# The preparation of a linear layer's weights in three float32r passes instead of one f32 pass, with GpSimd and VectorE splitting the operands

## The reference, cut to what matters

```python
x = x + L0(x)   # one expert per batch row (argmax of cond_8): silu(x wu + bu) * (x wg + bg), then wd, bd
x = x + L1(x)   # x W_base^T + b_base + 2 * sum_e cond[b,e] * (x As[e]^T) Bs[e]^T
x = x + L2(x)   # below
x = x + L3(x)   # two experts per batch row, weighted, gelu(x g) * (x u) then d; and a shared expert

def _L2_cond_ref(x, y, weight, mask, bias):
    masked_w = weight * mask[None, :, :]
    w_bot = jnp.einsum('bg,got->bot', y, masked_w)
    return jnp.einsum('bnt,bot->bno', x, w_bot) + bias
```

## Time and profile before

| | |
|---|---|
| median of 3 runs | 153.5 us (153.43 to 153.65) |
| the profiled execution | 153.69 us, of which 151.7 us are the span of its instructions |
| TensorE (PE) busy | 147.4 us, 97% of the span |
| VectorE (DVE) busy | 109.8 us, 72% |
| ScalarE (ACT) busy | 72.0 us, 47% |
| GpSimd (POOL) busy | 91.4 us, 60% |

### The profile page before, as it was taken

The page is one execution under the profiler, slowest core; times in us unless marked ns, Lnnn a source line. Parts: engine busy times, 40 slices in busy tenths (PEclk is TensorE's granted clock), DMA queues, the critical chain, the costliest instruction groups (busy, mean ns, idle before and its releaser), DMA issues.

```text
span 151.7 us, 3108 instructions
## 1 busy us (share of the span) xinstructions
PE 147.4 (97%) x1075; PEld 135.1 (89%) x1075; DVE 109.8 (72%) x229; ACT 72.0 (47%) x138; POOL 91.4 (60%) x93
## 2 busy tenths in 40 slices
PE   7999999999999999999999999999999999999992
PEld 2479999999978999999989999999999999999881
DVE  3985666667996586867775967876587895968772
ACT  2875444461375554454444354545425434345640
POOL 1003999999700007849994939995876999880000
PEclk9999999999999999999999999999999999999999
DMA  2999999974354676393397386095447047000052
GB/s 62 414 401 403 411 405 394 420 298 144 154 190 138 175 160 225 78 302 109 78 309 252 130 269 215 0 300 206 190 134 280 4 139 274 4 4 0 0 209 72
DMA packets 13912, 30.15 MB, mean 199 GB/s; under 512 B 1337, under 2 KB 8009, under 8 KB 13769
## 3 DMA queue, kind: packets, MB, share of 16 engines
q1 hardware_dynamic: 13472, 28.76, 54.7%
q10 hardware_dynamic: 424, 1.20, 2.0%
HBM read 24.71 MB, written 1.05 MB: 170 GB/s over the span
## 4 chain that ended last, share of the span: by engine, by line
PE 89%; DVE 4%; POOL 3%; ACT 2%; issue 1%; ACTq 0%; DVEq 0%; POOLq 0%
PE pair L550 22%; PE pair L540 12%; PE acc L599 10%; PE pair L482 10%; PE pair L557 8%; PE acc L584 6%; PE acc L608 5%; PE acc L490 5%; PE acc L438 2%; PE pair L526 2%; PE pair L497 2%; POOL duo_lo L372 2%; PE pair L471 2%; PE pair L445 2%; DVE hid L771 2%; ACT hid_hi L431 2%
## 5 line engine op out<-in xcount | busy, mean ns | idle before, releaser
L372 POOL TENSOR_TENSOR duo_lo<-raw_duo,duo_hi 128x512 fp32r<-128x512 f32 x36 | 48.6, 1350 | 2.9
L762 DVE TENSOR_TENSOR hid_lo<-hid,hid_hi 128x512 fp32r<-128x512 f32 (+1 forms) x41 | 36.1, 882 | 17.8 <-ACT hid_hi L431 17.3
L431 ACT ACTIVATE hid_hi<-hid 128x512 fp32r<-128x512 f32 (+1 forms) x41 | 25.4, 621 | 44.0 <-DVE hid L771 41.1
L369 POOL CAST duo_hi<-raw_duo 128x512 fp32r<-128x512 f32 x36 | 28.3, 786 | 28.5 <-PE acc L599 28.5
L771 DVE TENSOR_TENSOR hid<-pair,act 128x512 f32<-128x512 f32 (+1 forms) x49 | 32.9, 673 | 5.7 <-PE pair L550 4.2
L550 PE MATMUL pair<-x_duo,duo_hi 128*128 128x256 f32 x192 | 35.2, 281 | 0.2 <-POOL duo_lo L372 0.2
L412 ACT ACTIVATE act<-pair 128x512 f32<-128x512 f32 x48 | 28.3, 590 | 9.7 <-PE pair L550 7.7
L550 PEld LDWEIGHTS pair<-x_duo,duo_hi 128*128 128x128 f32 x192 | 29.7, 189 | 0.8 <-issue 0.3
L550 PE MATMUL pair<-x_duo,duo_lo 128*128 128x256 f32 x96 | 26.9, 280 | 0.0
L540 PE MATMUL pair<-x_hl,shared_hi 128*128 128x512 f32 x64 | 20.5, 401 | 0.1
L550 PEld LDWEIGHTS pair<-x_duo,duo_lo 128*128 128x128 f32 x96 | 18.0, 188 | 0.0
(11 more groups left out here) (101 smaller groups left out, 199.2 us busy)
## 6 DMA issues: line engine op xcount, KB each, us to landing
raw_duo<-experts SPq DMA_DIRECT2D x12, 768.0 KB, 5.2
ring<-experts SPq DMA_DIRECT2D x16, 386.5 KB, 6.7
raw_solo<-experts SPq DMA_DIRECT2D x8, 768.0 KB, 5.3
x_duo<-x_hl SPq DMA_DIRECT2D x24, 128.0 KB, 4.0
x<-xT ACTq DMA_DIRECT2D x1, 1024.0 KB, 6.2
lora_raw<-x SPq DMA_DIRECT2D x4, 256.0 KB, 2.4
raw_solo<-shared SPq DMA_DIRECT2D x1, 768.0 KB, 9.8
out<-lora_raw SPq DMA_DIRECT2D x3, 256.0 KB, 2.8
```

Of the source, the lines that this page charges most:

```text
L369: pool.tensor_copy(duo_hi[:, j % HALVES, piece(n)], raw_duo[:, j % RAWS, piece(n)])\
L372: pool.tensor_tensor(duo_lo[:, j % HALVES, piece(n)], raw_duo[:, j % RAWS, piece(n)], duo_hi[:, j % HALVES, piece(n)].bitcast(F32), ALU.su ...
L431: act.activation(hid_hi[:, k % SPLITS, at], hid3[:, u % PAIRS, at], ACT.Copy)\
L762: dve.tensor_tensor(hid_lo[:, k % SPLITS, at], hid3[:, u % PAIRS, at], hid_hi[:, k % SPLITS, at].bitcast(F32), ALU.subtract).then_inc(hid_ ...
```

## The change

The eight f32 matmuls become 24 in float32r, three for each k. GpSimd splits `w2_sb` in quarters of two k (128 x 256): a cast to the high part, then a subtraction for the low part. It does this before it waits for `slots_done`. VectorE splits `y_delta`: a copy, then a subtraction, in front of the routing chain. TensorE waits for VectorE's low part once, and for GpSimd's low part of each quarter. The parts lie in tiles that the last layer uses much later (`duo_hi`, `duo_lo`, `x_duo`).

```diff
@@
+        w2_hi = duo_hi[:, 0, 0:E * P].rearrange("p (k n) -> p k n", k=E)
+        w2_lo = duo_lo[:, 0, 0:E * P].rearrange("p (k n) -> p k n", k=E)
+        y_hi, y_lo = x_duo[:, 0, 0, :], x_duo[:, 0, 1, :]
@@ gpsimd
             pool.tensor_copy(earlier_b[:, :], cond_sb[:, EARLIER:EARLIER + B]).then_inc(ones_set, 1)
 
+            pool.wait_ge(w2_in, 16)
+            for n in range(E // 2):
+                at = slice(2 * n, 2 * n + 2)
+                pool.tensor_copy(w2_hi[:, at, :], w2_sb[:, at, :]).then_inc(w2_hi_done, 1)
+                pool.wait_ge(w2_hi_done, n + 1)
+                pool.tensor_tensor(w2_lo[:, at, :], w2_sb[:, at, :], w2_hi[:, at, :].bitcast(F32), ALU.subtract)\
+                    .then_inc(w2_lo_done, 1)
+
             pool.wait_ge(small_in, 16)
             pool.wait_ge(slots_done, 1)
@@ tensor
-            pe.wait_ge(ydelta_done, 1)
-            pe.wait_ge(w2_in, 16)
+            pe.wait_ge(ylo_done, 1)
             for k in range(E):
                 n = G + k // 2
                 if k % 2 == 0:
                     pe.wait_ge(prep_copied, n - len(prep) + 1)
-                ins = pe.matmul(prep[n % 3][:, (k % 2) * B * R:(k % 2 + 1) * B * R], w2_sb[:, k, :],
-                                y_delta[:, :, :].rearrange("p b j -> p (b j)"), start=True, stop=True)
+                    pe.wait_ge(w2_lo_done, k // 2 + 1)
+                for m, (w, y) in enumerate(((w2_hi, y_hi), (w2_hi, y_lo), (w2_lo, y_hi))):
+                    ins = pe.matmul(prep[n % 3][:, (k % 2) * B * R:(k % 2 + 1) * B * R], w[:, k, :], y,
+                                    start=(m == 0), stop=(m == 2))
                 if k % 2 == 1:
                     ins.then_inc(prep_mm, 1)
@@ vector
             dve.wait_ge(small_in, 16)
-            dve.tensor_tensor(y_delta[:, :, :], cond_rep[:, :].unsqueeze(2).to_broadcast([P, B, R]),
-                              small_sb[:, DELTA:DELTA + R].unsqueeze(1).to_broadcast([P, B, R]), ALU.mult)\
+            delta = small_sb[:, DELTA:DELTA + R].unsqueeze(1).to_broadcast([P, B, R])
+            dve.tensor_tensor(y_delta[:, :, :], cond_rep[:, :].unsqueeze(2).to_broadcast([P, B, R]), delta, ALU.mult)\
                .then_inc(ydelta_done, 1)
+            y = y_delta[:, :, :].rearrange("p b j -> p (b j)")
+            dve.wait_ge(ydelta_done, 1)
+            dve.tensor_copy(y_hi, y).then_inc(yhi_done, 1)
+            dve.wait_ge(yhi_done, 1)
+            dve.tensor_tensor(y_lo, y, y_hi.bitcast(F32), ALU.subtract).then_inc(ylo_done, 1)
 
             dve.wait_ge(exp_done, 1)
```

More of the change, by code:

```diff
@@ L218, in build_kernel @@
         ydelta_done, bsw_done = sem("ydelta_done"), sem("bsw_done")
+        yhi_done, ylo_done, w2_hi_done, w2_lo_done = (
+            sem("yhi_done"), sem("ylo_done"), sem("w2_hi_done"), sem("w2_lo_done"))
         prep_mm, prep_copied = sem("prep_mm"), sem("prep_copied")
```

## The result

The changed kernel takes **156.11 us** (155.83 to 157.34, 4 runs) against 153.57 us before (153.43 to 154.0, 4 runs): 1.0176 times as long, with an interval of 1.0117 to 1.0235; between the medians lie 2.5 us. The direction was right. The size was not: 8.2 us more were forecast (161.7). The median lies 0.1 us inside the stated range, which began at 156; that is luck, since the range was drawn for a reload of 3 us or more. What happened is rival 1, 0.6 us above the number it gave for its second form (155.5).

The account below looks back on a forecast made before the run. TensorE bounds the kernel, VectorE 0.8 us behind; an 8.2 us GpSimd reload delays the first subtraction, so TensorE's preparation ends at 20.2 instead of 11.94 us. Median 153.5 plus 8.2 gives 161.7 us; range 156 to 165, 8 in 10.

Parts of the forecast that it names:

- a reload of 3 us or more: GpSimd's MODIFY_POOL_CONFIG, moved from 2.7 to 6.4 us behind the first cast; main case priced from about 3 (156.5) to 11.1 us.
- rival 1: Reload free; GpSimd's splits hold VectorE's routing chain through port exclusion, so slot matmuls wait: 154.8 or 155.5 us; chance 0.11.
- its second form: Rival 1 with VectorE's two-element tensor_scalar operations in the routing chain held up as well: 155.5 us.
- I take 8.2: Reload's price before GpSimd's first subtraction, the middle of 6.7 to 9.8 us that DMA transfers starting then take to land.
- bounds of 0 and 11.1 us: Limits on the reload's price: library already resident, or all of GpSimd's idle time from 2.72 to 13.84 us.
- the seven idle microseconds of TensorE: TensorE was to idle from 8.5 us, waiting for GpSimd's first quarter, whose subtraction would end at 15.38.
- the 0.6 us for its clock: Addition for TensorE's lower clock level after idling during the float32r matmuls; bounds nothing to 1.5 us.
- the lumps of 1.2 to 1.4 us: Sign: TensorE's float32r preparation comes in four lumps that far apart, the first ones at twice the later price.
- its seven operations: Rival 1's held VectorE operations: y_delta, the copy, y_lo, pair_sum, pw_all, reached, even_odd; 0.2 us each on average, 1.3 in all.
- TensorE's gain of 0.65 us: Eight f32 matmuls, 3.46 us, become 24 float32r ones, 2.81 us; worth nothing at best because VectorE's payload ends later.
- a reload of 11.1 us: Upper end of the main case, the reload filling GpSimd's idle time: 164.8 us.
- 0.84 for a price that no row showed: Chance of the main case, a reload that holds GpSimd for some microseconds.

Follow-up runs that it names:

- e3: Changed kernel with a tiny 16x16 GpSimd addition in front of the wait for the weights, putting the reload back near 2.5 us: 156.01 us, before 153.83.
- e2: Kernel before plus only VectorE's copy and subtraction of y_delta, whose parts nobody reads: 154.12 us, before 153.83.
- e6: Changed kernel with ScalarE making w2's high part, GpSimd keeping only the four subtractions: 156.76 us, before 154.14.
- e4: Changed kernel with the slot matmuls moved behind batch 1 of the first layer: 155.14 us, before 153.83.
- e7: Changed kernel with ScalarE making w2's and y's high parts, slot matmuls behind batch 1, VectorE's subtraction behind pair_sum: 154.41 us, before 154.14.
- e9: Changed kernel with ScalarE making w2's high part, plus eight matmuls of zeros on TensorE before the payload wait: 155.47 us, before 154.09.
- e1: Kernel before plus only GpSimd's four quarter splits of w2, which nobody reads; TensorE keeps its f32 matmuls: 155.21 us, before 153.83.
- e8: Kernel before plus GpSimd's unread split of w2 as one cast and one subtraction of 1024 columns: 155.73 us, before 154.14.
- e5: Kernel before with only the slot matmuls moved behind batch 1 of the first layer: 153.99 us, before 154.14.

## Why the prediction was wrong

**The step that failed** is "I take 8.2" for the reload: bounds of 0 and 11.1 us, and a middle taken from transfers that had nothing to do with it. The operation behind it started 0.09 us (the changed kernel) and 0.04 us (e3) after the one in front had ended. The row of before had only shown room for a cost, not a cost. That the instruction would stand behind the first cast was right, and the words on what would refute it ("the first subtraction starts right behind its cast") were met. With it fell the seven idle microseconds of TensorE, the 0.6 us for its clock, and the lumps of 1.2 to 1.4 us. What stood in its place is a wait that the forecast had left out of its sum: VectorE's payload was to end near 13 us, long before L506; it ended at 14.68, and L506 waited for it.

**Rival 1 was right, in the form that gave 155.5.** It had 0.11, and named what came: the payload ends last, because GpSimd's operations hold VectorE's. Its sum, by its own steps: VectorE's two new operations cost 0.72 us (e2), 0.67 was taken; the copy was 0.29 and not 0.2. The holds come to 1.90 us in the changed kernel: y_delta 0.20, the copy 0.41, the subtraction 0.08, probs 0.29, pair_sum 0.14, pw 0.38, pw_rest 0.15, reached 0.25 (each against its duration in e2). With 1.3 for the operations that read two SBUF operands, or some 2.0 with the `tensor_scalar` operations, the second form is the one. Together 0.72 + 1.90 = 2.62, of the 2.66 measured. The split is not quite the rival's: 1.08 us for its seven operations (pw_all and even_odd weren't held), 0.82 for the `tensor_scalar` ones. "Where a VectorE operation reads two SBUF operands" was too narrow: probs, pw and pw_rest have one tensor operand, and so has the copy.

**What was right.** TensorE's gain of 0.65 us is worth nothing, since the payload ends last. GpSimd's durations (0.40 and 0.73) and the end of its quarters (10.86, forecast 10.5 to 10.9) came as worked out. The slot matmuls wait for the payload, and everything behind them moves by one constant (1.94 to 1.98 us). The difference of the medians, 2.5 us, is 0.4 above the 2.1 us between the profiled executions; the changed kernel's runs spread by 1.5 us. Two sums are off by a little, and nothing hangs on it: seven holds of 0.2 us are 1.4 and not 1.3, and a reload of 11.1 us gives 164.6 from the median, not 164.8.

**The weights of the cases.** Rival 1 rested on rows (0.35 us lost, 128 partitions), the forecast on a name. 0.84 for a price that no row showed was the error of judgement; the likeliest case should have been the one whose price was in the trace.

## What to carry to other kernels

GpSimd's idle time is not free when VectorE beside it runs a latency chain: each GpSimd operation can hold a VectorE operation, however small, for all the time that it still runs (RECIPROCAL, TENSOR_REDUCE and the copy out of PSUM weren't held here), so cost such a move as the number of GpSimd operations under the chain times what is left of each, and put it on ScalarE, or behind the chain, first. Before giving an instruction a price, look for a row in which something waits for it; a row that lies in idle time gives an upper bound and nothing more. And a wait in front of TensorE can cost 1.3 to 1.6 us more in clock, in some runs (e3) or in all (e6); with other matmuls moved into it (e4, e7), or matmuls on zeros (e9), no run showed the lower mean clock.

## What was unexpected of the hardware

- MODIFY_POOL_CONFIG costs nothing that can be seen in its queue: 0.09 us from the cast's end to the operation behind it at 6.4 us, 0.04 us at 2.5 us.
- Operations on 16 x 1 and 16 x 2 numbers are held for up to 1.90 us by one GpSimd subtraction (probs: 2.12 us against 0.22 alone). RECIPROCAL and the copy out of PSUM took 0.14 and 0.16 us beside GpSimd's subtractions.
- An idle stretch of 1.88 us was followed, 1.5 us after work had begun again, by 3.4 us at the lower clock level, in 6 runs of e6 out of 6 by their mean clock; in e3 the same mean clock stands in 2 of 6, the profiled one, with 1.90 us of idling, not among them. In e4 and e7, with waits of 0.99 and 1.07 us, it never came, but in e1 and e8, with 0.52 and 1.11 us in their profiles, in 2 of 6 each. It cost 1.3 us (e9 against e6) to 1.6 us (the pieces of the chain).
- When the matmuls at the start of the kernel reach their full speed differs between profiles with the same instructions by up to 1.4 us (7.1 us in e5, 8.5 in the changed kernel, by the last weight load of `prepare1`). The kernel before, 153.22 to 155.07 us in 74 runs, spreads by as much: its 18 runs with a mean clock of 0.998 or 0.999 took 153.22 to 153.63, the 56 with 1.000 had a median of 154.2. That the one makes the other wasn't tested.
